# A graph network of four layers: incidence rows prepared earlier, adjacency turned by DMA, bias added by GpSimd

## The reference

```
layer 0: deg = sum over rows of adj;  x += (deg^-0.5 * adj.T * deg^-0.5) @ (h @ W0) + b0
layer 1: inc = adj + mask/sqrt(count)   (mask: adj > 0, count: per row)
         x += (inc @ h) / sum(inc)
layer 2: 4 heads; ht = h @ W2; e = leaky_relu(src_i + dst_j, 0.01) + adj
         x += mean over heads of softmax(e) @ ht
layer 3: x += relu(adj @ (sign+(h) @ sign(W3).T))
```

## Time and profile before

| | us |
|---|---|
| median of 3 executions | 754.05 (753.78 to 754.13) |
| the profiled execution | 754.57 |
| its span | 752.8 |

### The profile page before, as it was taken

How to read it: one execution, slowest core, us unless ns; L and a number is a source line. 1 busy time by engine, 2 the same in 40 slices (tenths; PEclk the granted TensorE clock), 3 DMA queues, 4 the chain that set the end, 5 groups by cost and what they waited for, 6 DMA issues and landing times.

```text
span 752.8 us, 16841 instructions
## 1 busy us (share of the span) xinstructions
PE 731.1 (97%) x6816; PEld 622.8 (83%) x6816; DVE 648.9 (86%) x1196; ACT 485.9 (65%) x893; POOL 62.6 (8%) x102
## 2 busy tenths in 40 slices
PE   4999999999999999999999999999999999999998
PEld 3665888898889999546888888888888888888887
DVE  6788896868888886489999999999999999997683
ACT  4897020277677775587655877768696886766751
POOL 3004120211111110000000000000000000000000
PEclk7898999999999999999999999999999999999999
DMA  8886590055556633775011812135111713126691
GB/s 330 302 297 226 80 236 17 2 173 212 206 212 232 232 150 141 236 175 166 1 30 32 241 25 42 29 81 172 30 30 29 204 50 58 25 64 194 224 391 57
DMA packets 44173, 105.98 MB, mean 141 GB/s; under 512 B 3072, under 2 KB 17984, under 8 KB 39616
## 3 DMA queue, kind: packets, MB, share of 16 engines
q1 hardware_dynamic: 39824, 94.94, 36.4%
q0 software_dynamic: 4272, 9.96, 7.9%
HBM read 78.12 MB, written 18.91 MB: 129 GB/s over the span
## 4 chain that ended last, share of the span: by engine, by line
PE 83%; DVE 8%; ACT 6%; DMA 2%; issue 1%; SPq 0%; DVEq 0%; ACTq 0%
PE ps L746 15%; PE ps L747 15%; PE ps L748 15%; PE ps L686 4%; PE ps L788 3%; PE ps L789 3%; PE ps L582 3%; PE ps L581 3%; PE ps L580 3%; PE ps L609 3%; PE ps L633 2%; PE ps L635 2%; PE ps L634 2%; PE ps L613 2%; ACT arena L823 2%; DVE arena L1260 2%
## 5 line engine op out<-in xcount | busy, mean ns | idle before, releaser
L746 PE MATMUL ps<-arena 128*128 128x257 f16 x1024 | 280.0, 273 | 0.0
L748 PE MATMUL ps<-arena 128*128 128x257 f16 x1024 | 279.4, 273 | 0.0
L747 PE MATMUL ps<-arena 128*128 128x257 f16 x1024 | 279.3, 273 | 0.0
L1070 ACT ACTIVATE arena<-arena 128x512 f16<-128x512 f32 x252 | 158.5, 629 | 93.9 <-PE ps L748 61.9
L1393 DVE SCALAR_TENSOR_TENSOR arena<-arena,w_j 128x512 f32<-128x512 f32 x256 | 190.1, 744 | 0.0
L1400 DVE TENSOR_TENSOR arena<-arena 128x512 f16<-128x512 f32 x256 | 175.6, 687 | 3.7 <-ACT arena L1070 3.5
L747 PEld LDWEIGHTS ps<-arena 128*128 128x128 f16 x1024 | 100.3, 98 | 12.6
L748 PEld LDWEIGHTS ps<-arena 128*128 128x128 f16 x1024 | 99.8, 97 | 13.0
L746 PEld LDWEIGHTS ps<-arena 128*128 128x128 f16 x1024 | 99.9, 98 | 12.7
L633 PE MATMUL ps<-arena 128*128 128x257 f16 x256 | 70.3, 275 | 0.0
L635 PE MATMUL ps<-arena 128*128 128x257 f16 x256 | 69.7, 272 | 0.0
(11 more groups left out here) (154 smaller groups left out, 1183.8 us busy)
## 6 DMA issues: line engine op xcount, KB each, us to landing
arena<-in_adj_dram SPq DMA_DIRECT2D x32, 512.0 KB, 5.8
arena<-in_adj_dram SPq DMA_DIRECT2D x16, 1024.0 KB, 5.1
adj_t<-arena SPq DMA_DIRECT2D x16, 1024.0 KB, 5.5
arena<-adj_t SPq DMA_DIRECT2D x64, 256.0 KB, 4.1
arena<-adj_t SPq DMA_DIRECT2D x16, 1024.0 KB, 6.5
x<-arena POOLq DMA_DIRECT2D x15, 512.0 KB, 4.8
arena<-u_rows SPq DMA_DIRECT2D x4, 1024.0 KB, 13.6
x<-in_x_dram SPq DMA_DIRECT2D x4, 512.0 KB, 5.8
```

The costliest lines, as they stand in the source:

```text
L746: mm(ps[:, bank, 0:DE], hi, ht_hi[:, head, j, 0:DE], start=s, stop=False)
L747: mm(ps[:, bank, 0:DE], hi, ht_lo[:, head, j, 0:DE], start=False, stop=False)
L748: ins = mm(ps[:, bank, 0:DE], lo, ht_hi[:, head, j, 0:DE], start=False, stop=e)
L1070: nc.scalar.activation(p_hi[:, j % 4, :], prob[:, j % 4, :], copy).then_inc(p_hi_done, 1)
```

## The change

- **The parts of adj go to DRAM.** In layer 0 SyncE stores all of `nat` (16 stores of 1 MB) to `nat_dram`, row by row of `adj`. Nothing of `adj` is turned by TensorE, copied by ScalarE (L892) or stored from layer 1 any more.
- **adj is turned by DMA.** `turn_adj(n)` transposes a 512x512 block, high and low part (two DMA transposes of 512 KB, float16, DRAM to SBUF). Block n = 4q + g holds the columns of quarter q. GpSimd then writes the high part to `adj_t` in DRAM, cast to float32, and adds the low part there by a second, accumulating DMA. Blocks 0 to 3 are done in layer 1, 4 and 5 after it, the rest after the head sums of groups 0, 1, 2, 4 and 5. `adj_t` now holds adj times 256, so the exps scale it and layer 3 no longer does.
- **Five incidence rows in layer 0.** Rows 0 to 4 are masked, counted, filled and split in layer 0 on untransposed data and turned by DMA (SBUF to SBUF). Rows 5 to 15 are turned by TensorE, row t+4 between the products of row t, over three PSUM banks. The mask is now ScalarE's Sign and Relu; only three row buffers are left.
- **Moved.** The reductions of W2 with `a`, the low part of W2 and the maximum over partitions go from layer 0 to layer 1 and behind it; the first four exps from before the ht products into them; the two early splits of layer 3 from quarters 1 and 2 to quarter 3, after all of `adj_t` is there.
- **The bias** is loaded once and added to `x` by GpSimd, tile by tile, after the first normalisation has read the tile.

```diff
+        COUNTS = (1, 2, 9, 10, 11, 14)
+        FILLS = (3, 4, 11, 12, 14)
+        HIGHS = (4, 7, 12, 13, 15)
+        LOWS = (5, 8, 13, 14)
+        AHEAD = 5
+        WIDEN_AFTER = {0: (6, 7), 1: (8, 9), 2: (10, 11), 4: (12, 13), 5: (14, 15)}
...
+            def turn_adj(n):
+                q, g = n // TG, n % TG
+                if n >= 2:
+                    sp.wait_ge(wide[(n - 2) % TG], 16 * ((n - 2) // TG + 1))
+                slot = (turn_l1 if q == 0 else turn_l2)[n % 2]
+                for part in range(2):
+                    sp.dma_start_transpose(out=slot[:, part, :, :],
+                                           in_=nat_dram[TG * P * g:TG * P * (g + 1), part, QB * P * q:QB * P * (q + 1)]
+                                           ).then_inc(turned[n % 2], 16)
...
+            for k, (lo, hi) in enumerate(SENT):
+                for b in range(lo, hi):
+                    sp.dma_start(nat_dram[b * P:(b + 1) * P], nat[:, b, :, :, :].rearrange("p a j n -> p a (j n)")
+                                 ).then_inc(nat_sent[k], 16)
...
             sp.wait_ge(ht_ps, 2 * NB)
-            for i in range(2):
-                sp.dma_start(adjt_early[i], adjt_dram[i]).then_inc(adjt_in[4 + i], 16)
+            for n in range(QB, 3 * QB):
+                turn_adj(n)
             for q in range(1, NQ):
+                if q == 2:
+                    for n in range(3 * QB, 4 * QB):
+                        turn_adj(n)
...
                 load_e(q)
...
+            pool.wait_ge(bias_in, 16)
+            for t in range(NB):
+                pool.wait_ge(relu0, t + 1)
+                nc.gpsimd.tensor_tensor(x[:, t, :], x[:, t, :], b0_bc, ALU.add).then_inc(bias_added, 1)
...
+            def widen_high(n):
+                pool.wait_ge(turned[n % 2], 32 * (n // 2 + 1))
+                nc.gpsimd.dma_start(wide_rows(n), turned_slot(n)[:, 0, :, :]).then_inc(wide_hi, 16)
+
+            def add_low(n):
+                pool.wait_ge(wide_hi, 16 * (n + 1))
+                nc.gpsimd.dma_start(wide_rows(n), turned_slot(n)[:, 1, :, :], accum_op=ALU.add
+                                    ).then_inc(wide[n % TG], 16)
...
                 nc.gpsimd.dma_start(x[:, QB * q:QB * (q + 1), :], head_out[:, :, :], accum_op=ALU.add
                                     ).then_inc(head_added, 16)
+                for n in WIDEN_AFTER.get(group, ()):
+                    widen_high(n)
+                    add_low(n)
...
+                    if AHEAD <= t + 4 < NB:
+                        transpose_group(t + 4, g)
                     products1(t, g)
```

More of the change, by code:

```diff
@@ L266, in gnn_stack @@
         inc_lo_done = sem("inc_lo_done")
-        adjt_copied = sem("adjt_copied")
-        adjt_sent = [sem(f"adjt_sent{b}") for b in range(2)]
+        inc_in = [sem(f"inc_in{k}") for k in range(5)]
+        turned = [sem(f"turned{b}") for b in range(2)]
+        wide_hi = sem("wide_hi")
+        wide = [sem(f"wide{g}") for g in range(NB // TG)]
         l1_ps = sem("l1_ps")
@@ L672, in _ @@
                         h2_transposes(t - 2)
-                    if g == 3 and t >= 2:
-                        if t == 2:
-                            pe.wait_ge(wa_done, 1)
+                    if g == 3 and t == 6:
+                        pe.wait_ge(wa_done, 1)
+                        for k in range(4):
+                            scores(k)
+                    if g == 3 and t >= 6:
                         scores(t - 2)
@@ L908, in count @@
             def count(t):
-                act.wait_ge(masked, t + 1)
-                nc.scalar.activation(mask[:, t % 2, :], mask[:, t % 2, :], copy, accum_out=cnt[:, t:t + 1]
+                act.wait_ge(signed, t + 1)
+                nc.scalar.activation(mask[:, t % 2, :], mask[:, t % 2, :], ACT.Relu, accum_out=cnt[:, t:t + 1]
                                      ).then_inc(counted, 1)
-            for t in range(NB - 4):
+            for t in range(NB):
                 h1_high(t)
-                if t in (3, 4, 9):
-                    count((3, 4, 9).index(t))
@@ new lines, in _ @@
+                if t in HIGHS:
+                    inc_high(HIGHS.index(t))
+            act.wait_ge(nat_sent[5], 80)
+            for t in range(NB):
+                more = AHEAD <= t + 4 < NB
+                if more:
+                    part_high(t + 4, 0)
+                if t + 6 < NB:
+                    sign(t + 6)
+                if more:
+                    part_high(t + 4, 1)
+                if t >= 2:
+                    h2_turned(t - 2)
+                if more:
+                    part_high(t + 4, 2)
+                if t >= 1:
+                    h2_high(t - 1)
+                if more:
+                    part_high(t + 4, 3)
+                if t + 6 < NB:
+                    count(t + 6)
+                if t == 0:
+                    act.wait_ge(w2_in, 32)
+                    act.wait_ge(y_ps, NB)
+                    nc.scalar.activation(w2_hi, w2_f, copy, scale=W_SCALE).then_inc(w2_hi_done, 1)
@@ L951, in _ @@
             h2_turned(NB - 1)
-            for j in range(4):
-                exp_adj(0, j)
             act.wait_ge(d_shift, 1)
@@ L967, in ht_high @@
             def ht_high(t):
-                if t == 0:
-                    for b in range(2):
-                        act.wait_ge(adjt_sent[b], 16 * NB // 2)
                 for h in range(HEADS):
@@ L977, in _ @@
             act.wait_ge(exps, 3)
+            for g in range(TG):
+                act.wait_ge(wide[g], 16)
             ht_high(0)
@@ L1082, in head_high @@
                         exp_adj(q + 1, j - 8)
[L1083 to L1084 removed]
+                    if q == NQ - 1 and head >= 2 and j < 4:
+                        at3_high(head - 2, j)
                     if q == NQ - 1 and head == HEADS - 1 and j >= 12:
@@ L1293, in _ @@
-                if t == NB - 4:
-                    w2_a_parts()
+                if t in FILLS:
+                    fill(FILLS.index(t))
+                if t in LOWS:
+                    inc_low(LOWS.index(t))
             h1_low(NB - 1, 1)
@@ L1347, in _ @@
                 if more:
-                    inc_low(t + 1, 3)
-                if t + 3 < NB:
-                    fill(t + 3)
+                    part_low(t + 4, 1)
+                if t == 0:
+                    inc_low(4)
+                if t + 5 < NB:
+                    fill(t + 5)
+                if more:
+                    part_low(t + 4, 2)
+                    part_low(t + 4, 3)
                 if t >= 1:
@@ L1380, in _ @@
             v.tensor_scalar(w_j[:, :, :], w_j[:, :, :], P_SCALE, None, ALU.mult).then_inc(scaled_w, 1)
-            for b in range(2):
-                dve.wait_ge(adjt_sent[b], 16 * NB // 2)
+            for g in range(TG):
+                dve.wait_ge(wide[g], 16)
             vp_cols = vp_j[:, :, :].rearrange("p t h -> p h t")
```

369 lines of the change are left out of this document (197 added, 172 removed).

## The result

The changed kernel takes **767.81 us** (median of 4 runs, 766.15 to 771.09) against 754.09 (753.78 to 754.34) before: ratio 1.0188, interval 1.015 to 1.0225. It is slower by 1.9%; forecast were 745 and faster.

What follows compares the result with a forecast made beforehand. TensorE was taken to bound the kernel. From the median, 754.05 - 26 (layer 1 gain) + 17 (layer 2 loss, loads waiting for blocks) = 745; own range 738 to 752, over all cases 728 to 773.

Steps and rivals of the forecast that it cites:

- The rows of layer 1: Layer 1: rows 1 to 5 at 8.0 us, 6 to 11 at 7.6, 12 to 15 at 5.75, against 9.25 before.
- The hand-over from layer 0: Start of layer 1: the next transposes wait for the sixth fill, behind row 4's low part on VectorE, until 165.7.
- VectorE ... loss 1 us: Layer 0: VectorE's bunched load makes the last h1 low part at 159.4, wanted by TensorE at 158.6; loss 1 us.
- Layer 2's start: Layer 2: slots come free at 349.7, turning taken as 4.3 us, first block at 354 in the old clock.
- Six blocks and two sums: Layer 2, GpSimd's chain before quarter 1's loads: six blocks of 12.1 us and two head sums of 3.1, until 432.8.
- It is hidden later, since a block takes longer to widen: Layer 2: after the first block, turning, taken as 4.3 us, costs nothing beside a block's 12.1 us.
- rival B: Layer 2: the add costs by bytes, a block takes 15.5 us or more; loss 37, so 765; chance 0.21.
- Rival C: Layer 2: turning is slow, 13 us per MB; start and block 11 come 9 and 10 us later; 764; chance 0.10.
- a gap over 26 us: Before quarter 2 of layer 2 in ScalarE and TensorE: sign of B, or C if a transposed block exceeds 8 us.
- The tail: Layer 2, after the second sum: block 11 passes (3.0 us), then four loads land (about 5.6), until 441.4.
- The slack: Layer 2: ScalarE runs three steps, 4.0 us, ahead of TensorE, so the loss counts from 424.4, not 420.38.
- Quarter 2 and 3: 0: Layer 2: quarter 2 has its blocks by about 490, wanted at 505; quarter 3 has 40 us to spare; loss 0.

## Why the prediction was wrong, step by step

The terms were forecast as -26 and +17; the profile has -23.1 and +36.2, less 1.2 at the end. The mechanism named for layer 2 (SyncE's loads behind blocks 4 to 11, the wait of ScalarE, the gap of TensorE) is what happened. Its size was wrong by more than twice, and that turned the sign. Three steps failed: block 11's passing was priced as data only, turning was taken as hidden behind widening, and quarter 2 was put at nothing.

- **The rows of layer 1: the sum right, the first row wrong.** Forecast 8.0 us for rows 1 to 5, then 7.6, then 5.75. Row 1 took 11.4 us from its first transposes. Then came 8.12, 8.05, 8.04 and 7.57, for rows 6 to 10 7.3 to 8.6, for the last five 6.4, 6.3, 4.7, 5.67 and 5.66. The 3.4 us too many in row 1 are nearly made up later: from the first transposes to the end 110.3 us against 109.6. The 3 us for GpSimd's DMAs did not come.
- **The hand-over from layer 0: too early.** First transposes forecast at 165.7, measured at 171.06. Layer 0's first product is 1.5 us later than before (71.22 against 69.70). I put that down to GpSimd's late first selection (11.10 instead of 1.42), but the run with the late reduce alone has the same stand and no delay; what causes the 1.5 us is open. The rest is "VectorE ... loss 1 us": its last h1 low part is at 164.65, not 159.4, with a fill, a low part and a maximum in a row in front of it (5.85 us). TensorE waits 3.6 us for such parts, and 5.4 us more for the sixth fill. My walk row by row had the load right and its bunching too small. The wait costs a second time: from 171 to 176 us TensorE's granted clock is 0.50, where the kernel before has 1.00, and that is part of row 1's 11.4 us. With the point above: gain 23 instead of 26.

```profile
156.12 2.34 DVE L1361 SCALAR_TENSOR_TENSOR arena<-arena,c_row 128x2048 f32<-128x2048 f16 x1
158.39 2.29 DVE L1374 SCALAR_TENSOR_TENSOR arena<-arena 128x2048 f16<-128x2048 f32 x1
160.59 1.22 DVE L1317 TENSOR_TENSOR arena<-arena 128x2048 f16<-128x2048 f16 x1
```

```profile
171.06 0.69 PE L697 MATMUL ps<-ident,arena 128*128 128x128 f32 x2 [5.37 <-DVE arena L1361]
```

- **Layer 2's start: too early by 3.4.** From the first issue to the turned block I took 4.3 us; it took 7.65 (326.61 to 334.27). The first transpose takes SyncE 2.1 us to issue, and the second lands 5.2 us later. By line (issue on the engine in ns, min/median/max; below, with the same line, us to landing):

```profile
L383 SPq DMA_TRANSPOSE arena<-adj_parts x32: 1650/2374/5962, 196.4 to 504.7; - x32
...
DMA to landing us min/median/max: 4.2/6.3/10.0
```

- **Six blocks and two sums: right, by luck of two errors.** Forecast 78.8 us, measured 334.27 to 413.7, 79.4. I had added up casts, adds and sums one after another. From a cast's issue to that of its add it took 42.7 us for the six, where I had 30 (a cast lands in 7.5 us in the middle, not 5.0). But GpSimd issues the next cast without waiting for the add (341.33 and 342.12), so only the last add counts whole, 8.3 us. Between an add and the next cast lie 28.4 us. The two make 36.7 us, where I had 48.8 for adds and sums. Of the 28.4, GpSimd stood 19.7 for turned blocks: "It is hidden later, since a block takes longer to widen" failed. With two slots block 7's turning starts only when block 5 is widened and block 9's when block 7 is, 11.3 and 11.8 us each from issue to landing. Prediction's rival B did not decide: an add lands in 8.9 us, less than its 13.1 of transfer alone. Rival C did in part: by its sign, a gap over 26 us with a transposed block over 8 us in the queue, this case is nearer to C (764) than to the forecast. Its sizes were 9 us more at the start and 10 at block 11; measured were 3.4 and 3.8.
- **The tail: 16.5 us for 8.6.** This is the largest miss, 7.9 us. "Block 11 passes (3.0)" was priced as data moving; what passes is the time that SyncE's queue takes to issue two transposes, 6.8 us. And four loads land in 9.5 us beside that traffic, not 5.6.
- **The slack: 2.4 us came back, not 4.0**, and 1.6 more went in the half clock after the gap. I had no term for the clock. The two together with the three points before: 17 + 3.4 + 0.6 + 7.9 + 1.6 + 1.6 = 32.1.
- **"Quarter 2 and 3: 0" failed.** Blocks 14 and 15 are turned in front of quarter 2's loads, which leave at 507.55: 3.2 us there, 0.9 later. I had compared when quarter 2's blocks are ready, not what stands before the load in SyncE's list.
- **The bias: put at 0, 1.5 us in its own run.** The stores of 16 MB cost nothing, as said: one landed in 25.8 us (median), and TensorE is busy all 89 us from 69 to 158.
- **The rules weighed.** The prediction set the Trainium skill's figure for one DMA (DMA: Bandwidth & Descriptors, Anatomy of one DMA: 2.0 us plus bytes at 436 GB/s, 8.8 us a block) against the trace. The runs side with the trace: 13.2 us a block, the waits for turning included. And the estimate of 42 us a block, worked out from the Trainium skill's time of one 128x128 by DMA (VectorE: DVE Perf Modes, The three transpose paths), did not come either: the first block's two transposes of 512 KB were turned in 7.65 us, later ones in 11.3 and 11.8.
- **Row numbers.** The prediction names two groups the wrong way round: the 80 GB/s stand in the earlier trace rows, the queues' MB and shares (94.94 MB, 14.7%) in the earlier trace rows. The numbers are right.

The time lies inside the range, near its upper end of 773, and above the 764 and 765 of rivals C and B; slower had a chance of 0.37.

## What to carry to other kernels

A transfer that is moved into a queue costs three things: its data, the issuing engine's own time, and what is queued behind it; list each queue in order of issue with the time at which each entry is wanted, and let nothing stand before a load that waits for something the load does not need. Do it for all queues that touch the same buffers at once: the right order on one of them alone moved the wait to the other (757.4), and both by due time took 34 us off the same work (733.75). Before a second slot or a third is counted as overlap, add up the shares of the DMA engines in that stretch: at 112% a third slot brought 5 us of the 20 expected. A full share is no loss by itself, as the 108% of the fast version show; it is one where something waits for the end of the chain.

## What the hardware showed that I had not expected

- A DMA transpose of 512 KB took SyncE's queue 1.65 to 5.96 us to issue, median 2.37, where 16 plain loads of 256 KB were issued in 10.03 us, 0.6 each. For those from the arena to the arena it was 1.76 to 14.9. No view shows how much of that is work and how much is waiting for room.
- The transposes moved in packets of some 252 bytes; by the queue's share they took the sixteen engines 5.1 us per MB in the change and 5.9 with three slots, waiting in a packet's time included.
- GpSimd stood 9.5 to 10.4 us in front of its first selection, at the start of the program, in every version whose all-reduce comes late in the program, and 0.31 us where it comes in layer 0. What it does in that time no view shows, and in the run with the late reduce alone it did not delay layer 0.
- After 30 us without work TensorE ran its next products at half clock (1.2 of 2.4 GHz) for 3.4 us. At the start of layer 1 it had been busy 4.1 of 13 us, the last 5.4 idle, and the granted clock was 0.50 for the next 5 us.
